# Gated cross-attention block on one core: the last batches' steps reordered on TensorE, ScalarE and VectorE

## What is computed

```python
# x, ctx: (128, 128, 256); mask: (1, 1, 128, 128)
q = (layernorm(x) @ Wq + bq).reshape(N, 128, 16, 16)
k = (ctx @ Wk + bk).reshape(N, 128, 16, 16)
v = (ctx @ Wv + bv).reshape(N, 128, 16, 16)
energy = where(mask == 0, finfo.min, einsum('nqhd,nkhd->nhqk', q, k))
attn = softmax(energy / sqrt(16), axis=-1)
o = einsum('nhqk,nkhd->nqhd', attn, v).reshape(N, 128, 256) @ Wo + bo
x = x + tanh(g_xattn[0]) * o
x = x + tanh(g_ffn[0]) * tanh(layernorm(x) @ weight @ aux_weight1 @ aux_weight2 + bias)
```

## Time and profile before

| | us |
|---|---|
| median of three runs | 1086.19 |
| the runs | 1086.58, 1086.19, 1082.15 |
| the profiled execution, own time | 1082.12 |
| its span, first to last instruction | 1080.3 |

### The profile page before, as it was taken

The page is one execution under the profiler, slowest core; times in us unless marked ns, Lnnn a source line. Parts: engine busy times, 40 slices in busy tenths (PEclk is TensorE's granted clock), DMA queues, the critical chain, the costliest instruction groups (busy, mean ns, idle before and its releaser), DMA issues.

```text
span 1080.3 us, 45335 instructions
## 1 busy us (share of the span) xinstructions
PE 1032.1 (96%) x18487; PEld 895.7 (83%) x18487; DVE 950.4 (88%) x1331; ACT 828.6 (77%) x1275; POOL 799.9 (74%) x1184
## 2 busy tenths in 40 slices
PE   5988999999999999999999999999999999999965
PEld 5777888888888888888888888888888888888755
DVE  5778989999999999989899989999999999998865
ACT  4466878788888878878788778887888878888742
POOL 5245787778878787878787878788788787878753
PEclk9899999999999999999999999999999999999997
DMA  5134555656555555555555555556555555655432
GB/s 154 45 96 114 156 152 152 171 146 171 148 161 156 157 166 143 168 149 150 164 151 163 154 143 169 148 158 168 152 161 149 161 156 146 172 148 148 124 123 69
DMA packets 260400, 158.87 MB, mean 147 GB/s; under 512 B 174945, under 2 KB 227170, under 8 KB 260194
## 3 DMA queue, kind: packets, MB, share of 16 engines
q1 hardware_dynamic: 260050, 155.72, 51.4%
q10 hardware_dynamic: 144, 0.26, 0.1%
HBM read 85.92 MB, written 68.94 MB: 143 GB/s over the span
## 4 chain that ended last, share of the span: by engine, by line
PE 66%; SPq 10%; DMA 9%; issue 5%; DVE 5%; POOL 4%; ACT 0%; POOLq 0%; DVEq 0%; ACTq 0%
PE ps_m L507 13%; PE ps_m L500 13%; PE ps_s L636 10%; PE ps_s L615 10%; PE ps_x L647 8%; PE ps_m L574 7%; DMA scratch_y<-yn 4%; PE ps_s L621 3%; SPq L215 3%; DMA q_aug<-scratch_m 2%; DMA scratch_m<-max_T 2%; SPq L303 2%; PE ps_m L494 2%; SPq L292 1%; DVE probs L1021 1%
## 5 line engine op out<-in xcount | busy, mean ns | idle before, releaser
L1021 DVE TENSOR_TENSOR probs<-ps_s,far_T 128x2048 f32<-128x2048 f32 x128 | 293.3, 2291 | 53.9 <-PE ps_s L636 53.7
L1010 DVE TENSOR_REDUCE neg_max<-ps_s 128x16 f32<-128x2048 f32 x128 | 291.3, 2276 | 34.3 <-PE ps_s L621 34.1
L810 ACT ACTIVATE probs<-probs 128x2048 f32<-128x2048 f32 x128 | 245.0, 1914 | 5.8 <-DVE probs L1021 5.7
L615 PE MATMUL ps_s<-k_aug,q_aug 32*128 32x128 f32 x4096 | 150.7, 283 | 12.3 <-DVE probs L1021 8.2
L636 PE MATMUL ps_s<-q_aug,k_aug 32*128 32x128 f32 x4096 | 151.9, 284 | 7.0 <-DMA q_aug<-scratch_m 4.8
L615 PEld LDWEIGHTS ps_s<-k_aug,q_aug 32*128 32x128 f32 x4096 | 126.6, 186 | 31.0 <-issue 13.0
L636 PEld LDWEIGHTS ps_s<-q_aug,k_aug 32*128 32x128 f32 x4096 | 127.6, 187 | 25.0 <-DMA q_aug<-scratch_m 6.6
L785 ACT ACTIVATE q_aug<-ps_m,q_bias,q_scale 128x256 f32<-128x256 f32 x256 | 123.5, 563 | 27.2 <-PE ps_m L500 14.6
L785 ACT ACTIVATE k_aug<-ps_m,k_bias,parity 128x256 f32<-128x256 f32 x256 | 123.6, 563 | 26.2 <-PE ps_m L500 26.0
L647 PE MATMUL ps_x<-probs,v_ones 128*32 128x128 f32 x4096 | 139.2, 277 | 3.0 <-issue 2.2
L429 POOL TENSOR_TENSOR aT<-a_norm,aT 128x512 fp32r<-128x512 f32 x61 | 77.9, 1276 | 75.3 <-ACT aT L760 75.3
(11 more groups left out here) (123 smaller groups left out, 1788.2 us busy)
## 6 DMA issues: line engine op xcount, KB each, us to landing
scratch_a<-a_den SPq DMA_DIRECT2D x64, 512.0 KB, 3.5
x_in<-in_x SPq DMA_DIRECT2D x64, 256.0 KB, 4.3
a_rows<-scratch_a SPq DMA_DIRECT2D x64, 256.0 KB
den_wide<-scratch_r SPq DMA_DIRECT2D x64, 256.0 KB
out<-y SPq DMA_DIRECT2D x64, 256.0 KB, 4.6
ctx_in<-in_ctx SPq DMA_DIRECT2D x252, 64.0 KB, 2.7
scratch_y<-yn SPq DMA_DIRECT2D x59, 256.0 KB, 4.0
y_blocks<-scratch_y SPq DMA_DIRECT2D x236, 64.0 KB, 2.4
```

What stands on the lines that cost most here:

```text
L615: nc.tensor.matmul(ps_s[:, j, s, :], q_aug[p % 2][rows, n, s, :], k_aug[p % 2][rows, n, s, :], start=(s == 0), stop=False, tile_position=( ...
L810: nc.scalar.activation(tile, tile, ACT.Exp).then_inc(probs_ready, 1)
L1010: nc.vector.tensor_reduce(neg_max[:, 0:H].rearrange("p (j c) -> p j c", j=G), ps_s[:], AX.X, ALU.max, negate=True).then_inc(max_ready, 1)
L1021: nc.vector.tensor_tensor(probs[i % 2][:].rearrange("p j s q -> p (j s) q"), ps_s[:].rearrange("p j s q -> p (j s) q"), far_T[:].unsqueeze ...
```

## The change

Within the last round of the loop (t = 63) and behind it, steps change places; no instruction is added or removed.

- TensorE: in the last round scores_T(127) goes ahead of make_f(58), weigh_values(125) goes behind scores_T(126), and make_o(63) goes ahead of make_f(60).
- ScalarE: tanh(58) goes behind exponents(127), and keep_a(127) ahead of high_of_y(59).
- VectorE: mask_transposed(126) goes ahead of low_of_y(58); mask_transposed(127) is first behind the loop; divide_last_a(61) goes ahead of bias_f(58); reciprocals(63) goes ahead of add_residual(61); divide_last_a(63) and low_of_last_a(63) go ahead of finish_last(59) and low_of_y(60); add_residual, moments and the norm of pair 63 go ahead of low_of_y(61) and finish_last(60), and bias_f(60) is done within this norm, in place of bias_f(61).

```diff
@@ TensorE, loop @@
-                        if t == NP - 1:
-                            weigh_values(i - 2)
...
+                        if t == NP - 1:
+                            weigh_values(i - 2)
+                            scores_T(i)
                         if is_pair(t + 1):
                             make_v(t + 1, 1)
@@ TensorE, behind the loop @@
-            scores_T(NB - 1)
             weigh_values(NB - 2)
...
             make_o(y1)
             turn_y(y3)
+            make_o(last)
             make_f(y3)
             turn_y(y2)
-            make_o(last)
             make_f(y2)
@@ ScalarE @@
             exponents(NB - 2)
-            tanh(END)
             keep_a(NB - 2)
             exponents(NB - 1)
+            tanh(END)
             high_of_a(y2)
+            keep_a(NB - 1)
             high_of_y(y4)
-            keep_a(NB - 1)
@@ VectorE, loop @@
                     reciprocals(t - 2)
+                if t == NP - 1:
+                    mask_transposed(2 * t)
                 if is_pair(t - 5):
                     low_of_y(t - 5)
...
-                if is_batch(2 * t):
+                if t < NP - 1:
                     mask_transposed(2 * t)
@@ VectorE, behind the loop @@
+            mask_transposed(NB - 1)
             reciprocals(y1)
+            divide_last_a(y2)
             bias_f(END)
-            mask_transposed(NB - 1)
-            divide_last_a(y2)
             add_residual(y3)
...
             divide_last_a(y1)
+            reciprocals(last)
             add_residual(y2)
             moments_of_y(y2)
-            reciprocals(last)
             low_of_last_a(y1)
             bias_f(y4)
             add_residual(y1)
+            divide_last_a(last)
             moments_of_y(y1)
+            low_of_last_a(last)
             finish_last(y4)
             low_of_y(y3)
-            divide_last_a(last)
-            bias_f(y3)
-            low_of_last_a(last)
+            add_residual(last)
+            moments_of_y(last)
+            normalise_last_y(last, y3)
             low_of_y(y2)
             finish_last(y3)
-            add_residual(last)
-            moments_of_y(last)
-            normalise_last_y(last, y2)
+            bias_f(y2)
             low_of_y(y1)
```

## The result

The changed kernel takes 1090.42 us (median of 15 runs, 1085.64 to 1094.06), the kernel before 1083.23 us (median of 15, 1078.99 to 1090.39). The ratio of the two is **1.0045, with a 95% interval of 1.0026 to 1.0063**: slower by about 4.9 us.

A forecast was written before the change was run, and what follows sets the result against it. It took TensorE as no longer the bound in the last 49 us, with mask(127) stalled 2.57 us. Terms summed to +4.2 us, giving 1086.3 or 1090.3 by run level; it put 1088.0, range 1081.1 to 1093.5.

The forecast's parts named there:

- The sum, +4.2: All terms of the last round and behind it together: the span grows by 4.2 us, from 1080.3 to 1084.5.
- Front, keep_a(127) 0.2 us early: Last round up to keep_a(127): the last pair gains only 0.2 us, or 0.7 with the clock held.
- Reciprocals(63) 0.9 us early: VectorE behind the loop: den lands 4.1 us after issue, so reciprocals(63) start at 1051.5 instead of 1052.38.
- Reciprocals to read_wide 1.78 us: From reciprocals(63) to read_wide behind the loop: 1.78 us, the spacing taken from the profile before.
- low_of_last_a(63) 2.1 us early: VectorE behind the loop: no longer waiting for bias_f(60), low_of_last_a(63) ends at 1060.4 instead of 1062.56.
- turn_y(61) holds GpSimd, the norm 1.3 late: GpSimd behind the loop: normalise_y(62) waits for turn_y(61), delaying pair 63's power; norm ends at 1070.4, not 1069.1.
- low_of_y(61) behind the norm: End of the kernel: make_f(61) and later steps queue behind it; norm to last make_f takes 9.3 us instead of 6.3.
- From there to the end 4.83 us, and nothing of that changes.: Behind the last make_f: bias, tanh, gate and store take 4.83 us, unchanged.
- The clock holds: Rival for the last round and behind it: each step keeps its short duration, +1.0 us; chance 0.20.
- The last pair's lead is kept: Rival behind the loop: waits on turn_y(61) and low_of_y(61) are hidden, -2.1 us, bounds 0 and -3; chance 0.12.
- Slower beyond: Rival: TensorE stays slow after the 3.8 us idle, make_f(58) over 2.5 us; +5.6 to +8 us; chance 0.18.
- the change does nothing: Rival: q_aug and den hold the path as before and the late steps are hidden; chance 0.05.

The follow-up runs named there:

- e6: Changed kernel with low_of_y(60) back ahead of divide(63), make_f(60) and turn_y(61) back ahead of make_o(63); among three runs timed at 1.0013 to 1.0016 of the kernel before.
- e12: Kernel before with only low_of_y(61) and finish(60), then bias_f(61), moved behind the norm of pair 63; ratio 1.0032 (1.0006 to 1.0059).
- e2: Changed kernel with low_of_y(61) done within the norm of pair 63 instead of behind it; ratio 0.9998 to the kernel before.
- e8: Changed kernel plus 20 unread matmuls in the wait ahead of scores_T(127); among three runs timed at 1.0013 to 1.0016 of the kernel before.
- e11: Changed kernel plus 36 unread matmuls in the wait ahead of make_f(61); 12.98 us from the norm to the end of the span.
- e5: Changed kernel plus 24 unread matmuls in the wait ahead of make_f(61); among three runs timed at 1.0013 to 1.0016 of the kernel before.
- e3: Kernel before with only the front half of the change (scores, weighings, masks, divide(61), ScalarE's order); ratio 0.9965 to the kernel before.
- e4: Kernel before with only the late half of the change (reciprocals, division, make_o and norm of pair 63 earlier); ratio 1.0047 to the kernel before.
- e10: Kernel before with the front half, weighings and some pair-63 steps earlier, pair 58's store behind write_reciprocals(63), 20 unread matmuls ahead of scores_T(127); ratio 0.9996.
- e1: Changed kernel with make_f(58) put back ahead of scores_T(127) on TensorE; ratio 1.0075 to the kernel before.

## Why the prediction was right

**The sum, +4.2 against a measured +4.17 in the stretch, and +4.9 timed.** The time, 1090.42, fell inside the range and the sign was right, and the loss arose where the forecast had put it. The verdict is "same" by the bound of 0.5% that the forecast set, by a little: the interval reaches 1.0063. That the sum fits to 0.03 us is luck. The norm of pair 63 came 0.7 us late where 1.3 had been forecast, the time behind the last make_f grew by 0.7 where nothing had been, and identical code differs by more than that from one profile to the next.

**Its terms, one by one:**

- *Front, keep_a(127) 0.2 us early.* Measured 0.0 (15.06 against 15.07). scores_T(127) took 2.09 us, not 1.65: I took the length of other matmuls that came after the clock had fallen, in part at the high level. make_f(58) took 2.20 against the 2.3 taken, and 1.69 to 2.93 in other executions of the same code; make_o(60) started at 11.81 against 11.5 forecast.
- *Reciprocals(63) 0.9 us early.* Wrong size: 2.4 (18.10 against 20.49). den landed 2.4 us after its issue, not 4.1. The 4.1 of pair 62 was taken with a store of pair 57 issued 0.56 us ahead; that this made it longer is likely but not shown. VectorE stood 0.37 us there, not the 2 us that the forecast named as a sign.
- *Reciprocals to read_wide 1.78 us.* Wrong too, and it took the gain back: 1057.52 - 1054.12 = 3.4 us. The chain of the changed kernel shows why (start, length, what):

```profile
1052.96 0.41 SPq L267
...
1053.42 1.56 SPq L309
...
1055.07 2.43 DMA scratch_r<-den_r
1057.51 0.02 issue
1057.52 4.44 DMA den_wide<-scratch_r
```

  and the same write in the kernel before:

```profile
1052.73 1.41 DMA scratch_r<-den_r
```

  Earlier reciprocals meet write_a(63) and the store of pair 58 on SyncE's queue: the issue of the store took 1.56 us (1.10 before), the small write 2.43 instead of 1.41. So divide(63) was 0.8 early, with 0.7 forecast: two errors of 1.5 and 1.6 cancelled.
- *low_of_last_a(63) 2.1 us early.* 1064.25 - 1036.02 against 1062.56 - 1031.89, that is 28.23 against 30.67: 2.4.
- *turn_y(61) holds GpSimd, the norm 1.3 late.* The mechanism is in the trace (normalise_y(62) behind it, VectorE idle 1.74 us for the power); the size was 0.7. e6 puts the step at 0.7 to 1.4.
- *low_of_y(61) behind the norm.* From the norm's end to that of the last make_f 9.3 us were forecast and 1083.10 - 1073.95 = 9.15 came. e12 and e2 show that this is the cause.
- *"From there to the end 4.83 us, and nothing of that changes."* Wrong: 1088.6 - 1083.10 = 5.50. With both last make_f at full clock, the input of bias_f(63) was ready at 1083.10, but the step stood behind finish(62) in VectorE's list and began at 1083.79; before, it waited for make_f(63).

**The rivals.** "The clock holds" fell in the profile, and e8 and e11 show its price: 1.4 us in front, 1.7 late. 4.17 less both is 1.1, close to the +1.0 that the rival gave; no run has the clock held in both places. It explains what the changed kernel would have gained, not why it lost: the kernel before paid 1.8 us of the same kind behind its norm. The rule of the Trainium skill ("TensorE: Matmul & The Clock Gate", Part 1: under 1% of a span) fits the two pieces priced here, 1.4 and 1.7 us, together 0.3% of the span; the rest of the span wasn't priced. It is of no use for a change of this size. "The last pair's lead is kept" fell in the profile: the 2.4 us of low_of_last_a(63) are gone at the end of the norm, 0.7 late. "Slower beyond" was to be decided by a make_f(58) of over 2.5 us. It took 2.20 in the changed kernel's profile, but 2.93 in e5, e6 and e11, with the same code up to there, and keep_a(127) came 0.6 to 1.3 us later than in that profile. So the rival's condition comes and goes from one execution to the next, and its further 2.4 us at the end did not come: the last two make_f took 1.67 and 1.58 us. That the change does nothing is out with e3 and e4: its halves do opposite things.

## What to carry to other kernels

When a late batch is moved ahead on one engine, look at what stands in front of its *next* step on another: here make_f(61) stayed ahead of the turn of pair 63 on TensorE, while its input had been put behind that pair's norm on VectorE, and a single step of 0.7 us decided 3.5. A wait into which another step happened to fit costs that step's time when the step is taken out of it (make_f(58), 2.20 us ahead of the weighing), and the matmuls behind the longer idle time can run at the low clock as well (2.09 us instead of the 1.17 of e8). Before the price of an order is split into clock and queue, ask what clock the other order ran at. And a transfer that is released earlier meets other transfers on its queue; take its price from a row with the same neighbours, or keep a bound on both sides.

## What the runs showed of the hardware

- The length of an idle time alone doesn't tell the clock behind it. In e5 TensorE ran 24 matmuls in 3.12 us, stood 1.79 us, and the next make_f took 2.56 us (2.90 in the changed kernel after 4.66 us); the same wait filled to 0.36 us gave 1.66 (e11). But make_f(60), after 2.71 us idle in both, took 1.67 us in e12 (granted clock 1.00) and 2.90 in e10 (0.50):

```profile
1059.30 2.90 PE L507 MATMUL ps_m<-wf_s,yT 128*128 128x256 f32 x12 [2.71 <-DVE yT L979]
```

- A small DMA took longer close behind a large one, if not always. By the chains of waits the 16 KB of the reciprocals took 1.41 us where they were issued 3.4 us behind the store of pair 58 (256 KB; before), 2.0 at 2.1 us behind it (e3), 2.2 at 1.6 us (e4), 2.4 at 1.65 us (after), and in e1, 1.05 us behind it, 4.22; but e8, at the same 1.04 us, has 2.25.
- 63 rounds of identical code took up to 8.6 us more or less from one execution to the next (the landmark at 1031.2 to 1039.8 us), at a mean granted clock of 0.982 to 0.995 over the span. Two single profiles can't be compared by their spans at this size. A landmark ahead of the change takes this out, but not what identical code varies by behind it: 2.2 us up to keep_a(127), over five profiles. The time from the norm to the end repeated within 0.2 us in the six kernels with the new order and nothing put in ahead of make_f(61) (14.50 to 14.67), and spread over 1.8 us in the order of before (9.34 to 11.16), with the clock of the last two make_f.
